# Output projection over 128 rows with the mask on zero weights, and a gate with its 8 columns standing

## The chip, the cores and the metric

One core of one Trainium2 chip. The time is device microseconds (us) of one execution of the whole kernel; lower is better. The three timed executions of the kernel before took 962.52, 965.40 and 968.63 us.

## The reference

Four residual steps on `x` of shape (8, 128, 512), fp32: a grouped-query attention, a dense layer with four routed low-rank adapters, a patchwise attention, and a mixture of 8 experts of which each token takes 2. The change touches the third step's last product and the fourth step's gate:

```python
def _L1_xattn_ref(qk, v, masks, Wq, bq, Wk, bk, Wv, bv, Wo, bo):
    ...
    o = jnp.einsum('bhij,bhdj->bhdi', attn, vh).reshape(BN, DK, W)      # DK = 64
    o = jax.nn.gelu(o, approximate=False)
    out = jnp.einsum('de,bew->bdw', Wo, o) + bo[:, None]
    out = out.reshape(B, np_, D, W).transpose(0, 2, 1, 3).reshape(B, D, S)
    out = out * masks
    return out

def _L1_ffn_ref(x, W_gate, b_gate, W_e, b_e):
    TOP_K = 2
    logits = x @ W_gate + b_gate                                        # (8, 128, 8)
    _, top_idx = jax.lax.top_k(logits, TOP_K)
    y_all = jax.nn.relu(jnp.einsum('bsd,edh->bseh', x, W_e) + b_e)
    y = jnp.take_along_axis(y_all, top_idx[..., None], axis=2)
    return y.mean(axis=2)

x = x + jnp.tanh(g_xattn[1]) * _L1_xattn_ref(_layernorm(x), ctx, mask, ...)
x = x + jnp.tanh(g_ffn[1]) * _L1_ffn_ref(_layernorm(x), ...)
```

## The kernel before

`x` stays in SBUF as `X`, 8 batches of 128 tokens by 512. Each engine has its program written out by hand (a block each for SyncE `sp`, GpSimd `gp`, ScalarE `ac`, VectorE `ve`, TensorE `pe`); engines meet through semaphores, and an engine runs its own instructions in the order in which they are written. The four residual steps follow one another, and the loops inside run over batches.

The place of the change is the stretch between the patchwise attention and the experts. A batch passes through these steps there:

- ScalarE's `gelu(b)` (L866) works on `o_t[0:64, b, :]`, the 64 attention channels of a batch, and GpSimd's `masked(b)` (L626) multiplies them by the mask. Row 64 of `o_t` holds the mask itself (loaded by SyncE, L403), so that the bias row of the weights `wo1g` is masked as well.
- TensorE's `output(b)` (L1670) is one fp32 product over 65 rows into bank 2 or 3. In the trace it has two instruction records.
- VectorE's `attended(b)` adds it to `X` (L1210) and takes the statistics of the row (`row_stats`, L911 and L914); GpSimd's `row_scale` turns them into mean and 1/sigma (L496 to L499); `final_rows(b)` normalises into `h` or `h2` (L917). SyncE writes that out to `h_rows` (`keep_rows`, L449). From batch 4 on, `final_rows` waits until the first four batches are written out (`hrow_out`).
- TensorE's `turn_last(b)` transposes the normalised batch in four pieces (L1677), and ScalarE evicts it to `xt` (L877). After each such eviction ScalarE also rounds two pieces of the expert weights (`expert_hi`, L683).
- TensorE's `gate(b)` (L1683) multiplies each of the four pieces of `xt`, 128 by 128 and standing in the array, by 8 streaming columns of `wg`. The 128 by 8 logits of four batches lie side by side in one bank.
- VectorE, behind its last `final_rows`, copies `tri` (L1233), then runs `choose(0)` and `choose(1)` (L1240 to L1255), which rank the logits of four batches each. Then come the counting products (L1701 to L1709), the list of rows per expert tile, the gather from `h_rows` and the expert products.

TensorE's order is written out: outputs 0 to 2, then per turn `output(b)`, `turn_last(b - 3)`, `gate(b - 4)`.

Two other places are touched. VectorE makes `wo1g` inside the second step (L1181, in the turn of batch 3), and TensorE waits soon after it for `p_w` and `h`, which VectorE writes behind it (L917). SyncE's queue issues, in that order, the context load of batch 2 (L397), the copies of `stack(2)` (L421 to L430, for which the scores of batch 2 wait) and a load of expert weights (L407).

Of the kernel before, what the change touches and what calls it, by code (L numbers as in the profile page):

```python
# [46 lines left out]
def flamingo_gated_two_layers(nc, x, ctx, ctx_t, mask_tq, mask_b, g_xattn, g_ffn, wq0, wk0, wv0, wo0,  # L47
# [6 lines left out]
    with ExitStack() as stack:  # L54
# [69 lines left out]
        diag = sb("diag", [P, HG + 1])  # L124
        wo1g = sb("wo1g", [E1 + 1, P])
        wg = sb("wg", [P, KT, EX])
# [122 lines left out]
        mask_8 = over("mask_8", [B, D])  # L249
        o_t = sb("o_t", [E1 + 1, B, D])  # L250
        ctx_s = sb("ctx_s", [P, 2, D])
# [86 lines left out]
        def _(sp):  # L338
# [57 lines left out]
            def load_ctx(b, j):  # L396
                sp.dma_start(ctx_s[:, j, :], ctx[b]).then_inc(ctxs_in[j], 16)  # L397
# [3 lines left out]
            for b in range(B):  # L401
                sp.dma_start(mask_bb[:, b, :], mask_b[b, 0:1, :].to_broadcast([P, D])).then_inc(maskb_in, 16)
            sp.dma_start(o_t[E1:E1 + 1, :, :], mask_b.rearrange("b o d -> o b d")).then_inc(maskb_in, 16)  # L403
            sp.dma_start(mask_8[:, :], mask_b.rearrange("b o d -> (b o) d")).then_inc(pen_raw, 16)
# [31 lines left out]
            for b in range(2, B):  # L436
                sp.wait_ge(vc_mm, CREDIT + b - 1)
                load_ctx(b, b % 2)
                stack(b)
                if b - 2 < FIRST:  # L440
                    load_expert(b - 2)
# [42 lines left out]
        def _(gp):  # L484
# [139 lines left out]
            def masked(b):  # L624
                gp.wait_ge(gelu_ok, CREDIT + b + 1)
                nc.gpsimd.tensor_tensor(o_t[0:E1, b, :], o_t[0:E1, b, :], mask_bb[0:E1, b, :], ALU.mult).then_inc(om_ok, 1)  # L626

            masked(0)
            masked(1)
# [35 lines left out]
        def _(ac):  # L665
# [194 lines left out]
            def expert_hi(e, k):  # L860
                if k == 0:
                    ac.wait_ge(we_in[e], 16)
                hi_part(w_hi[:, e, k, :], w_raw[e][:, k, :], weh_ok)

            def gelu(b):
                nc.scalar.activation(o_t[0:E1, b, :], o_t[0:E1, b, :], ACT.Gelu).then_inc(gelu_ok, 1)  # L866
# [8 lines left out]
            for b in range(B):  # L875
                ac.wait_ge(ht_mm, CREDIT + 2 * B + b + 1)
                nc.scalar.activation(xt[:, :, b * P:(b + 1) * P], heads(ps[:, b % 2, :]), ACT.Copy).then_inc(hth_ok, 1)  # L877
                for n in range(2 * b, 2 * b + 2):
                    expert_hi(n // KT, n % KT)
# [23 lines left out]
        def _(ve):  # L903
# [273 lines left out]
            for b in range(2, B):  # L1177
                mix(b, b % 2, last=b == B - 1)
                row_stats(2, b - 2, b % 2, x2_ok)
                if b == 3:  # L1180
                    nc.vector.tensor_scalar(wo1g[:, :], wo1[:, :], tanh_g[0:E1 + 1, 1:2], None, ALU.mult).then_inc(wo1_ok, 1)  # L1181
                    nc.vector.memset(q3[PARTS:PARTS + 1, :, :, :].bitcast(F32), 1.0).then_inc(pen_ok, 1)
# [5 lines left out]
                if b == B - 5:  # L1188
                    ve.wait_ge(maskb_in, 16 * (B + 1))
                    rows(0, 0, p_w)  # L1190
                    kept(0, 0)
# [43 lines left out]
            def choose(half):  # L1235
# [3 lines left out]
                ve.wait_ge(gate_mm, CREDIT + 4 * half + 4)  # L1239
                nc.vector.tensor_tensor(gl[:, at, :], ps[:, 4 + half, 0:4 * EX].rearrange("p (b e) -> p b e", b=4),  # L1240
                                        bcast(bg[:, :], 4), ALU.add).then_inc(rank_ok, 1)
# [121 lines left out]
        def _(pe):  # L1363
# [316 lines left out]
            def gate(b):  # L1680
                pe.wait_ge(hth_ok, CREDIT + 2 * B + b + 1)
                for k in range(KT):
                    last = nc.tensor.matmul(ps[:, 4 + b // 4, b % 4 * EX:(b % 4 + 1) * EX], xt[:, k, b * P:(b + 1) * P], wg[:, k, :],  # L1683
                                            start=k == 0, stop=k == KT - 1)
                last.then_inc(gate_mm, 1)

            pe.wait_ge(wo1_ok, CREDIT + 1)
            for b in range(3):
                output(b, b % 2)
            for b in range(3, B + 3):  # L1690
# [3 lines left out]
                if b >= 4:  # L1694
                    gate(b - 4)
            gate(B - 1)

            pe.wait_ge(kz_ok, CREDIT + 1)
# [106 lines left out]
```

## Time and profile before

| what | us |
|---|---|
| median of three timed executions | 965.40 |
| lowest and highest of them | 962.52, 968.63 |
| the profiled execution, whole | 966.84 |
| its span in the trace | 965.0 |
| TensorE busy | 894.5 |
| VectorE busy | 619.6 |
| ScalarE busy | 325.0 |
| GpSimd busy | 404.5 |

All times inside the trace are counted from the start of the span of the one profiled execution; the 1.84 us between span and whole execution lie around it. TensorE's products overlap one another, so the length of a single record is longer than its step to the next one: where a rate matters, the chain of waits shows the step. PE in the views is TensorE, PEld its weight loads, DVE is VectorE, ACT ScalarE, POOL GpSimd, SPq the queue that SyncE issues to. PEclk is the granted clock of TensorE as a share of 2.4 GHz; 0.50 is 1.2 GHz.

### The profile page before, as it was taken

What the parts mean: (1) busy time and instruction counts of PE and PEld (TensorE: products, weight loads), DVE (VectorE), ACT (ScalarE), POOL (GpSimd) and SP (SyncE); (2) the same over time, 40 slices, a digit from 0 to 9 for tenths busy, and PEclk for the clock granted to TensorE, in tenths of its full rate; (3) what the DMA queues carried; (4) which work ended last, traced back from release to release, by engine and by line L of the source; (5) the groups of instructions that cost most, each with busy time, mean ns of one, the idle gap of its engine ahead of it and who ended that gap; (6) DMA issues with size and microseconds to landing.
All of it is one profiled execution on the core that took longest, in us unless ns stands there. A gap on an engine that the chain in (4) does not pass through costs nothing.

```text
span 965.0 us, 13870 instructions
## 1 busy us (share of the span) xinstructions
PE 894.5 (93%) x4771; PEld 728.3 (75%) x4771; DVE 619.6 (64%) x1067; ACT 325.0 (34%) x581; POOL 404.5 (42%) x417
## 2 busy tenths in 40 slices
PE   5999999999999999999999999988999998857993
PEld 4778878978878877877977877865888885745772
DVE  5975675375674276575376577578888875777345
ACT  4333143223133214124214124221665664612230
POOL 4651532251442153253153153337764606528551
PEclk9999999999999999999999999989999996559997
DMA  9020120020120011120011011202344205313448
GB/s 314 11 88 1 33 88 1 12 87 2 33 88 1 13 45 43 33 88 1 12 43 44 1 27 52 87 26 61 113 136 134 66 2 214 142 44 131 134 149 307
DMA packets 42242, 70.13 MB, mean 73 GB/s; under 512 B 7034, under 2 KB 14779, under 8 KB 42051
## 3 DMA queue, kind: packets, MB, share of 16 engines
q1 hardware_dynamic: 37060, 56.97, 18.1%
q0 software_dynamic: 3680, 12.06, 3.8%
q8 instruction: 43, 0.70, 0.3%
q10 hardware_dynamic: 1440, 0.24, 0.1%
q14 instruction: 19, 0.16, 0.1%
HBM read 52.61 MB, written 10.22 MB: 65 GB/s over the span
## 4 chain that ended last, share of the span: by engine, by line
PE 84%; DVE 8%; issue 3%; DMA 2%; ACT 1%; ACTq 1%; POOL 1%; DVEq 0%; SPq 0%
PE ps L1370 18%; PE ps L1372 18%; PE ps L1371 17%; PE ps L1491 6%; PE ps L1483 6%; PE ps L1620 5%; PE ps L1499 3%; PE ps L1608 3%; PE ps L1601 2%; PE ps L1670 1%; DMA rows_in<-h_rows,gather_i 1%; PE ps L1716 1%; PE ps L1628 1%; DVE h L917 1%; PE ps L1576 1%
## 5 line engine op out<-in xcount | busy, mean ns | idle before, releaser
L528 POOL TENSOR_TENSOR q_t<-rot_a,rot_b 128x512 f32<-128x512 f32 x64 | 82.7, 1291 | 152.8 <-DVE rot_b L962 152.8
L960 DVE TENSOR_TENSOR rot_a<-ps,cos 128x512 f32<-128x512 f32 x80 | 55.2, 689 | 87.2 <-PE ps L1372 86.6
L1370 PE MATMUL ps<-xt_hi,wq_hi 128*128 128x512 f32 x256 | 107.6, 420 | 0.5 <-DVE rot_b L962 0.5
L1370 PE MATMUL ps<-wo_hi,at_hi 128*128 128x512 f32 x256 | 106.7, 417 | 0.4 <-DVE at_lo L1068 0.4
L1372 PE MATMUL ps<-xt_hi,wq_lo 128*128 128x512 f32 x256 | 101.1, 395 | 0.0
L1371 PE MATMUL ps<-xt_lo,wq_hi 128*128 128x512 f32 x256 | 101.0, 394 | 0.0
L1372 PE MATMUL ps<-wo_hi,at_lo 128*128 128x512 f32 x256 | 100.2, 391 | 0.0
L1371 PE MATMUL ps<-wo_lo,at_hi 128*128 128x512 f32 x256 | 99.9, 390 | 0.0
L755 ACT ACTIVATE ps<-ps 128x512 f32<-128x512 f32 x64 | 37.2, 582 | 178.6 <-PE ps L1483 178.6
L768 ACT ACTIVATE at_hi<-ps 128x512 fp32r<-128x512 f32 x64 | 38.2, 597 | 171.7 <-PE ps L1499 171.7
L1073 DVE TENSOR_TENSOR X<-ps,X 128x512 f32<-128x512 f32 x64 | 44.2, 690 | 74.0 <-PE ps L1372 73.7
L592 POOL TENSOR_TENSOR k_blk<-k,diag 96x512 fp32r<-96x512 f32 x64 | 65.4, 1053 | 24.7 <-DMA k<-qk_lo 24.7
L502 POOL TENSOR_TENSOR wq_lo<-wq_raw,wq_hi 128x512 fp32r<-128x512 f32 x32 | 41.4, 1297 | 78.8 <-ACT wq_hi L683 78.8
L1370 PEld LDWEIGHTS ps<-wo_hi,at_hi 128*128 128x128 f32 x256 | 48.0, 187 | 30.3 <-DVE at_lo L1068 17.2
L1491 PE MATMUL ps<-v_ones,e_w 128*128 128x129 f32 x512 | 67.7, 275 | 0.0
L528 POOL TENSOR_TENSOR k_t<-rot_a,rot_b 128x512 f32<-128x512 f32 x16 | 20.7, 1294 | 108.5 <-DVE rot_b L962 108.5
L1620 PE MATMUL ps<-v_pad,p_t 128*128 128x72 f32 x512 | 64.8, 269 | 1.1 <-ACT p_t L836 1.0
L1068 DVE TENSOR_TENSOR at_lo<-ps,at_hi 128x512 fp32r<-128x512 f32 x64 | 44.2, 690 | 32.6 <-ACT at_hi L768 32.6
L1483 PE MATMUL ps<-q_t,k_t 128*128 128x512 f32 x128 | 64.1, 593 | 0.0
L1491 PEld LDWEIGHTS ps<-v_ones,e_w 128*128 128x128 f32 x512 | 62.8, 192 | 0.7
L1620 PEld LDWEIGHTS ps<-v_pad,p_t 128*128 128x128 f32 x512 | 62.2, 192 | 1.4 <-ACT p_t L836 1.1
L1051 DVE TENSOR_TENSOR e_w<-ps,cap 128x512 f32<-128x512 f32 x64 | 44.1, 689 | 28.8 <-ACT ps L757 28.5
(217 smaller groups left out, 2131.2 us busy)
## 6 DMA issues: line engine op xcount, KB each, us to landing
wq_raw<-in_wq SPq DMA_DIRECT2D x8, 1024.0 KB, 5.2
wo_raw<-in_wo SPq DMA_DIRECT2D x8, 1024.0 KB, 5.1
w_raw<-in_we SPq DMA_DIRECT2D x8, 1024.0 KB, 5.7
X<-in_x SPq DMA_DIRECT2D x4, 512.0 KB, 11.9
wk_raw<-in_wk SPq DMA_DIRECT2D x8, 256.0 KB, 2.9
q_t<-in_ctx_t SPq DMA_DIRECT2D x2, 1024.0 KB, 9.5
wv_raw<-in_wv SPq DMA_DIRECT2D x4, 512.0 KB, 3.7
ctx_s<-in_ctx SPq DMA_DIRECT2D x8, 256.0 KB, 4.2
```

The source lines that it names most:

```text
L528: nc.gpsimd.tensor_tensor(dst, rot_a[:, r % 2, :], rot_b[:, r % 2, :], ALU.add).then_inc(rope_ok, 1)
L592: nc.gpsimd.tensor_tensor(k_blk[0:PARTS, b % 2, g, patch, :, :], bcast(k3[0:PARTS, g, patch * P:(patch + 1) * P].bitcast(F32), HG), diag[0 ...
L960: nc.vector.tensor_tensor(heads(rot_a[:, r % 2, :]), heads(bank), bcast(cos[:, :], 4), ALU.mult)
L1051: nc.vector.tensor_tensor(heads(e_w[:, b % 2, :]), heads(ps[:, 2 + b % 2, :]), bcast(cap[:, :], G), ALU.min).then_inc(e_ok, 1)
L1068: nc.vector.tensor_tensor(at_lo[:, b % 2, :], ps[:, 6, :], at_hi[:, b % 2, :].bitcast(F32), ALU.subtract).then_inc(al_ok, 1)
L1073: nc.vector.tensor_tensor(X[:, b, :], ps[:, 7, :], X[:, b, :], ALU.add).then_inc(x1_ok, 1)
L1370: nc.tensor.matmul(dst, w_hi, x_hi, start=start and k == 0, stop=False)
L1371: nc.tensor.matmul(dst, w_hi, x_lo, start=False, stop=False)
L1372: last = nc.tensor.matmul(dst, w_lo, x_hi, start=False, stop=stop and k == n - 1)
L1483: nc.tensor.matmul(ps[:, 2 + b % 2, :], k_t[:, b * P:(b + 1) * P], q_t[:, :, b * P:(b + 1) * P], start=True, stop=True).then_inc(s_mm, 1)
L1491: last = nc.tensor.matmul(ps[:, 4 + n // 2, at:at + P + 1], e_w[:, b % 2, n * P:(n + 1) * P], v_ones[:, b, 1 if odd else 0, 0:P + 1], star ...
L1620: last = nc.tensor.matmul(ps[:, 6 + j, patch * VA:(patch + 1) * VA], p_t[:, u % 2, n * P:(n + 1) * P], v_pad[:, at:at + VA], start=head == ...
```

## The change

`o_t` and `wo1g` become 128 rows high. VectorE first clears rows 64 to 127 of `wo1g`, then writes rows 0 to 64 as before, so that rows 65 to 127 hold zeros. Rows 64 to 127 of `o_t` hold the mask, one copy from DRAM with 64 partitions as destination instead of one; it is issued later, behind the context load of batch 2, and counts on `pen_raw`, for which GpSimd now waits ahead of `masked(0)`. The product of `output(b)` runs over 128 rows.

The gate is turned round: `wg[:, k, :]`, 128 by 8, stands in the array and a batch's 128 columns of `xt` stream, which gives logits of 8 by 128 in bank 4 or 5. ScalarE evicts them to `r_d` (`gate_row`), and TensorE transposes that into the place in which `choose` wants them (`gate_columns`, now banks 6 and 7).

```diff
-        wo1g = sb("wo1g", [E1 + 1, P])
+        wo1g = sb("wo1g", [P, P])
...
-        o_t = sb("o_t", [E1 + 1, B, D])
+        o_t = sb("o_t", [P, B, D])
...
-            sp.dma_start(o_t[E1:E1 + 1, :, :], mask_b.rearrange("b o d -> o b d")).then_inc(maskb_in, 16)
...
                 load_ctx(b, b % 2)
+                if b == 2:
+                    sp.dma_start(o_t[E1:P, :, :], mask_b.rearrange("b o d -> o b d").to_broadcast([P - E1, B, D])).then_inc(pen_raw, 16)
                 stack(b)
...
+            gp.wait_ge(pen_raw, 32)
             masked(0)
...
+            def gate_row(b):
+                ac.wait_ge(ot_mm, CREDIT + B + b + 1)
+                nc.scalar.activation(r_d[0:EX, b // 4, b % 4 * P:(b % 4 + 1) * P], ps[0:EX, 4 + b % 2, 0:P], ACT.Copy).then_inc(ot_ev, 1)
...
                 nc.scalar.activation(xt[:, :, b * P:(b + 1) * P], heads(ps[:, b % 2, :]), ACT.Copy).then_inc(hth_ok, 1)
+                if b >= 1:
+                    gate_row(b - 1)
+                if b == B - 1:
+                    gate_row(b)
                 for n in range(2 * b, 2 * b + 2):
                     expert_hi(n // KT, n % KT)
...
-                    nc.vector.tensor_scalar(wo1g[:, :], wo1[:, :], tanh_g[0:E1 + 1, 1:2], None, ALU.mult).then_inc(wo1_ok, 1)
+                    nc.vector.memset(wo1g[E1:P, :], 0.0).then_inc(wo1_ok, 1)
+                    ve.wait_ge(wo1_ok, CREDIT + 1)
+                    nc.vector.tensor_scalar(wo1g[0:E1 + 1, :], wo1[:, :], tanh_g[0:E1 + 1, 1:2], None, ALU.mult).then_inc(wo1_ok, 1)
...
-                    ve.wait_ge(maskb_in, 16 * (B + 1))
+                    ve.wait_ge(maskb_in, 16 * B)
...
-                nc.vector.tensor_tensor(gl[:, at, :], ps[:, 4 + half, 0:4 * EX].rearrange("p (b e) -> p b e", b=4),
+                nc.vector.tensor_tensor(gl[:, at, :], ps[:, 6 + half, 0:4 * EX].rearrange("p (b e) -> p b e", b=4),
...
-                    last = nc.tensor.matmul(ps[:, 4 + b // 4, b % 4 * EX:(b % 4 + 1) * EX], xt[:, k, b * P:(b + 1) * P], wg[:, k, :],
+                    last = nc.tensor.matmul(ps[0:EX, 4 + b % 2, 0:P], wg[:, k, :], xt[:, k, b * P:(b + 1) * P],
                                             start=k == 0, stop=k == KT - 1)
-                last.then_inc(gate_mm, 1)
-
-            pe.wait_ge(wo1_ok, CREDIT + 1)
+                last.then_inc(ot_mm, 1)
+
+            def gate_columns(b):
+                pe.wait_ge(ot_ev, CREDIT + B - 1 + b + 1)
+                nc.tensor.transpose(ps[:, 6 + b // 4, b % 4 * EX:(b % 4 + 1) * EX], r_d[0:EX, b // 4, b % 4 * P:(b % 4 + 1) * P],
+                                    ident[0:EX, 0:EX]).then_inc(gate_mm, 1)
+
+            pe.wait_ge(wo1_ok, CREDIT + 2)
...
                 if b >= 4:
                     gate(b - 4)
+                if b >= 5:
+                    gate_columns(b - 5)
             gate(B - 1)
+            gate_columns(B - 2)
+            gate_columns(B - 1)
```

On TensorE, in the mixed stage (batches 6 and 7 of `output`; `h_149` is `h2`), there stood before:

```order
L1670 MATMUL ps<-o_t,wo1g 128x512 [waits x3_ok,om_ok]
L1677 MATMUL ps<-ident,h_149 128x128 [waits hth_ok,h_ok]
L1677 MATMUL ps<-ident,h_149 128x128 x3
L1683 MATMUL ps<-wg,xt 128x8 [waits hth_ok]
L1683 MATMUL ps<-wg,xt 128x8 x3
L1670 MATMUL ps<-o_t,wo1g 128x512 [waits x3_ok,om_ok]
```

and there stands now, at the same place:

```order
L1682 MATMUL ps<-o_t,wo1g 128x512 [waits x3_ok,om_ok]
L1689 MATMUL ps<-ident,h_149 128x128 [waits hth_ok,h_ok]
L1689 MATMUL ps<-ident,h_149 128x128 x3
L1695 MATMUL ps<-xt,wg 8x128 [waits hth_ok]
L1695 MATMUL ps<-xt,wg 8x128 x3
L1701 MATMUL ps<-ident,r_d 128x8 [waits ot_ev]
L1682 MATMUL ps<-o_t,wo1g 128x512 [waits x3_ok,om_ok]
```

The four gate products write 8 by 128 where they wrote 128 by 8, and one transpose, of the batch before, stands behind them ahead of the next output.

On ScalarE, the evictions of `xt` in the same stage with the expert weights between them (`w_raw_138` is expert 1), before:

```order
L877 ACTIVATE xt<-ps 128x4x128 [waits ht_mm]
L683 ACTIVATE w_hi<-w_raw_138 128x512 [waits we_in1]
L683 ACTIVATE w_hi<-w_raw_138 128x512
L877 ACTIVATE xt<-ps 128x4x128 [waits ht_mm]
L683 ACTIVATE w_hi<-w_raw_138 128x512 x2
```

and now:

```order
L883 ACTIVATE xt<-ps 128x4x128 [waits ht_mm]
L869 ACTIVATE r_d<-ps 8x128 [waits ot_mm]
L685 ACTIVATE w_hi<-w_raw_138 128x512 [waits we_in1]
L685 ACTIVATE w_hi<-w_raw_138 128x512
L883 ACTIVATE xt<-ps 128x4x128 [waits ht_mm]
L869 ACTIVATE r_d<-ps 8x128 [waits ot_mm]
L685 ACTIVATE w_hi<-w_raw_138 128x512 x2
```

Behind each eviction of `xt` stands one of a batch's logits, which waits for the gate of the batch before.

## Rows read from the trace of the kernel before

**Rows 1.** The page: busy time by engine, TensorE's granted clock by slice

```profile
PE 894.5 (93%) x4771; PEld 728.3 (75%) x4771; DVE 619.6 (64%) x1067; ACT 325.0 (34%) x581; POOL 404.5 (42%) x417
...
PEclk9999999999999999999999999989999996559997
```

**Rows 2.** Chain of waits: start us, us, engine, tile and line (x instruction records)

```profile
745.12 1.02 PE ps L1628 x8
...
752.84 0.86 PE ps L1576 x2
753.70 0.44 PE ps L1608 x4
...
801.20 1.92 PE ps L1628 x8
803.12 5.43 PE ps L1670 x6
...
814.94 1.51 PE ps L1683 x8
816.44 1.91 PE ps L1670 x2
...
826.92 0.70 DVE X L1210
...
831.42 1.21 DVE tri L1233
...
842.89 0.39 PE ps L1701
```

**Rows 3.** Stretches: length, busy PE PEld DVE ACT POOL (x), PEclk, DMA share, GB/s

```profile
671.70:675.00 3.30, 3.27 (x8) 2.06 (x9) 3.20 (x8) 0.55 (x1) 0.83 (x4) 0.50 0.34 86
675.00:680.00 5.00, 4.92 (x42) 4.52 (x41) 4.78 (x8) 3.61 (x7) 5.00 (x8) 1.00 0.34 91
676.80:683.80 7.00, 7.00 (x62) 6.74 (x60) 6.64 (x12) 4.79 (x10) 7.00 (x9) 1.00 0.13 39
803.10:808.60 5.50, 5.44 (x7) 1.75 (x6) 3.16 (x7) 0.59 (x1) 1.72 (x4) 0.50 0.74 246
811.00:838.40 27.40, 27.11 (x105) 22.36 (x104) 19.26 (x30) 14.68 (x28) 18.57 (x29) 0.50 0.41 155
```

**Rows 4.** Timeline of TensorE: start us, us, line, out<-in, shapes

```profile
672.29 1.91 PE L1576 MATMUL ps<-h,wqk 128*128 128x512 f32 x2
673.99 1.06 PE L1608 MATMUL ps<-ident,p_w 128*128 128x128 f32 x4
```

**Rows 5.** Groups by line, 801 to 843 us: count, busy us, mean ns, idle before

```profile
L917 DVE TENSOR_SCALAR h<-X,mean,rstd 128x512 f32<-128x512 f32 x8 | 5.9, 747 | 0.4 <-POOL rstd L499 0.4
L911 DVE BATCH_NORM_STATS2 stats<-X 128x6 f32<-128x512 f32 x8 | 5.6, 695 | 0.3
L1210 DVE TENSOR_TENSOR X<-ps,X 128x512 f32<-128x512 f32 x8 | 5.5, 690 | 11.4 <-PE ps L1670 11.3
...
L914 DVE BATCH_NORM_AGGREGATE mean_var<-stats 128x2 f32<-128x6 f32 x8 | 1.5, 182 | 0.3
```

**Rows 6.** Timeline of VectorE

```profile
811.13 0.68 DVE L1210 TENSOR_TENSOR X<-ps,X 128x512 f32<-128x512 f32 x1
...
839.39 0.18 DVE L1240 TENSOR_TENSOR gl<-ps,bg 128x32 f32<-128x32 f32 x1
```

**Rows 7.** DMA issues from 795 to 870 us: count, KB each, median us to landing

```profile
h_rows<-h SPq DMA_DIRECT2D x8, 256.0 KB, 2.2
```

**Rows 8.** VectorE, the line that clears a tile: ns min/median/max, start

```profile
L943 DVE MEMSET count<- x1: 72/72/72, 19.8 to 19.8; 128x16 f32 x1
```

**Rows 9.** VectorE, the line that writes wo1g

```profile
L1181 DVE TENSOR_SCALAR wo1g<-wo,tanh_g x1: 704/704/704, 637.0 to 637.0; 65x128 f32<-65x128 f32 x1
```

**Rows 10.** Timeline of SyncE's queue, its issues

```profile
676.32 0.52 SPq L397 DMA_DIRECT2D ctx_s<-in_ctx  x1
683.87 2.60 SPq L421 DMA_DIRECT2D k<-qk_hi  x4
```

## The prediction, made before the changed kernel was run

> **What bounds the kernel now.** I read four views in this order. First the page: TensorE is busy for 93% of the span, at the higher of its two clock levels, 2.4 GHz, almost everywhere; the three slices that say 6, 5, 5 lie between about 796 and 868 us [rows 1]. The reader is to see that the one long dip is exactly where the change works. Second, the chain of waits there: from 803.12 to 826.92 it is TensorE's (outputs L1670, transposes L1677, gate L1683), then VectorE's from its last addition of a projected batch at 826.92, through `tri` at 831.42, up to TensorE's L1701 at 842.89 [rows 2]. So what matters in this stage is when VectorE gets the last output, not when the last gate is done. Third, the table by stretches: the clock is 0.50 (1.2 GHz) from 803.1 to 838.4, although TensorE is busy for 5.44 of the first 5.50 us and nearly all the time afterwards [rows 3]. Fourth, the groups: L1210 of VectorE waits 11.3 us for TensorE in total and works 5.5 [rows 5]; the other engine has much room.
>
> What the clock did before it rose elsewhere is the key. At 671.7 it was at 0.50 too. Then came two records of a 128-row, 512-column fp32 product and 128-row transposes [rows 4], in a stretch with 3.27 of 3.30 us busy, and from 675 it is 1.00 [rows 3]. At 803.12 the same kind of product with 65 rows ran 5.43 us without a pause [rows 2], and nothing rose. The visible difference between the two is the rows: 128 against 65. This is an inference from one place each, not a proof.
>
> A rule of the Trainium skill speaks against the change: "TensorE: Matmul & The Clock Gate", Part 1 (The HAM clock gate), says that the gate follows how busy the array has been, with sustained back-to-back work releasing it, and names no rows. By that rule padding rows would buy nothing. The trace of 803.1 to 808.6 does not fit a rule of busy time alone, so I lean on rows; what the rule would give is the first rival. The same page, Part 4 (PE-mode transpose), says that transposes don't count as busy for the gate; no row here separates that, and it would leave outputs and gate alone to hold the clock.
>
> **The change, part by part.**
>
> *Outputs with 128 rows.* Eight products, each 2 records. At the low clock three of them took 5.43 us, 1.81 each; the number of rows does not set that: the 128-row product in rows 4 took 1.91 for its two records at the low clock, the 65-row one also 1.91, and the 128-row one 0.86 at the high clock [rows 2, 4]. So padding alone costs nothing, and the clock gives back 1.91 - 0.86 = 1.05 per output. I expect outputs 0 to 2 still at 1.2 GHz, with the rise near their end, about 808.
>
> *Gate turned round.* Before: 4 products with 8 columns streaming, 1.51 us per batch at 1.2 GHz [rows 2]. After: 4 products with 128 columns streaming. The nearest row is L1628, also 4 fp32 products of 128 columns: 1.92 us at 1.2 GHz and 1.02 at 2.4 [rows 2]. To this comes one small transpose per batch for the columns; its price is bounded by 0 and by the 0.44 that four 128x128 transposes take at the high clock [rows 2]; a quarter of that is 0.11, and I take 0.15, and 0.2 at the low clock. So a gate costs 1.17 at the high clock and 2.12 at the low one, 0.6 more than before. ScalarE gets an eviction of 8x128 per batch. It was busy for 14.68 of the 27.40 us from 811 to 838.4 [rows 3], and the eviction sits beside TensorE's next products, except after the last batch, where VectorE has not reached the second `choose` yet. Its price is not shown; bounds are the 0.18 of a tiny VectorE operation and the 0.69 of a 128x512 one [rows 5], and I take 0.3.
>
> *The rate per batch.* TensorE at 2.4 GHz: 0.86 + 0.44 + 1.02 + 0.15 = 2.47 us. Before, at 1.2 GHz: 1.91 + 2 x 0.44 + 1.51 = 4.30; the additions of batches 3 and 7 began 826.92 - 811.13 = 15.8 us apart, 3.95 a batch, since the first of the four has no gate ahead of it. VectorE: 0.69 + 0.70 + 0.18 + 0.75 = 2.32 [rows 5]. The two are almost level; 2.47 is the larger and sets the pace. VectorE's addition of batch 3 began at 811.13 [rows 6], and there it was VectorE's own work that was late, so it stays. Four more batches: 811.13 + 4 x 2.47 = 821.0 instead of 826.92, 5.9 us earlier. What is late next is VectorE, at 2.32. One wait could come forward: `final_rows(4)` needs the fourth copy into h_rows landed, 2.2 us after its issue [rows 7]; the fourth normalised batch is ready near 818, so landing near 820.5, about when VectorE comes to it: 0 to 0.5, held within the 5.9. If that cover were gone, each further microsecond of landing would be one of the time.
>
> *After the last addition.* The chain is VectorE's to 842.89 in both kernels: 16 us from 826.92, unchanged in work. The gates have to be done by `choose(1)`, 839.39 before [rows 6], which moves to 833.5; TensorE, with 1.17 + 0.44 per batch left, is done by about 830. TensorE then idles and falls back to 1.2 GHz as before; the routing and expert stage moves as a whole by 5.9 us.
>
> *The transfer.* The 1-row copy into `o_t` goes from SyncE's queue; a 64-partition one (1 MB) comes behind the context load of batch 2, issued at 676.32. SyncE's next issue was at 683.87 [rows 10], and the DMA engines were busy for 0.13 of 676.8 to 683.8 [rows 3]. At the rate of 803.1 to 808.6, where 246 GB/s kept the engines busy for 0.74 [rows 3], 1 MB needs 1 / 0.33 = 3.2 us and fits. Behind it on the queue stands `stack(2)`, on which scores of batch 2 hang; without that gap it would be up to 3 us later. I take 0. POOL's new wait before `masked(0)` is for this copy, which is some 120 us old by then: 0. Behind it on POOL stand all of `masked`, and thus all outputs.
>
> *memset of 64x128, and a wait, on VectorE* near 637, ahead of `p_w` and `h` for which TensorE waits soon after. Bounds: 0.07 (128x16 cleared) [rows 8] and 0.70 (all of wo1g) [rows 9]; I take 0.2, nearer to the first since it is a clear. It is on the path.
>
> **Sum:** -5.9 + 0.2 = -5.7 us. The profiled execution took 966.84 us (span 965.0 and 1.84 around it): 961.1. It lies 1.4 above the median of 965.4, so in the terms of the median 965.4 - 5.7 = 959.7, 0.6% faster.
>
> **Rivals.**
> 1. *The clock never rises (slower): the change doesn't do what it looks made to do.* Something other than the rows kept the clock at 0.50 from 803 on, and keeps it there. For it: the work before 803.12 and the wait behind it are the same in both kernels, and the mixed stage from 811 to 838.4 was busy for 27.11 of 27.40 us without a rise [rows 3]. Against it: the pair of places above. The Trainium skill's rule of busy time (above) gives the same outcome, since nothing is made busier. The price: 0.6 per gate. Three gates with their small transposes stand before the last addition, +1.8; all eight before `choose(1)`: TensorE's work reached to about 838.4 [rows 3], 1.0 us ahead of `choose(1)` [rows 6], so 8 x 0.6 + 0.3 for ScalarE's last eviction - 1.0 = 4.1 late, which takes in the 1.8. It decides from the point where the last gate is done after `choose(0)`. 965.4 + 4.1 + 0.2 = 969.7.
> 2. *It rises and falls again.* Outputs bring it up, then gates with 8 columns standing, or transposes, don't hold it. For it: a stage of transposes and gates never rose before (811 to 838.4 at 0.50) [rows 3]. Against: in the attention stage before, made of short products and transposes, the clock stayed at 9 tenths or more for four slices [rows 1], and every batch here still has a full output. At two of the four batches each way: gain 2.9, extra cost 2 x 0.6 = 1.2: 965.4 - 1.7 + 0.2 = 963.9.
> 3. *It rises at once, or never falls.* For it: the fall came only about 801, and where it comes may differ from one execution to another. Against: nothing in the change touches what went before 803. Output 0 is done 1.81 - 0.86 = 0.95 earlier, and VectorE, whose own work sets the pace from there to 811.13, starts that much earlier: 959.7 - 0.95 = 958.7.
>
> **How the numbers follow.** Forecast 0.65, rival 1 0.13, rival 2 0.12, rival 3 0.10. The forecast's own range: at best a batch costs 0.86 + 0.44 + 0.86, a gate priced like one output and no transpose, 2.16 x 4, 1.2 us more gained; at worst the clock rises one batch late, 1.8 us less: 958.5 to 961.5. The executions of before lie between 962.5 and 968.6, so 3 us either way are spread that no term explains. I give 956.0 to 967.5, which takes in rivals 2 and 3 and leaves out most of rival 1. A measurement of this kernel tells about 1% from no change. Over 1% faster means below 955.7, which needs more than VectorE's own pace allows: 0.1. Over 1% slower needs 975.1: 0.03. Within 1%: 0.87.
>
> **What would show it.** Right: granted clock 1.00 from about 808 to after 825, output records near 0.43 us apart instead of 0.9, gates near 1.0 us per batch, VectorE's last addition of a projected batch near 821, and L1701's counterpart near 837. Wrong: clock 0.50 up to 838 with gates of 1.9 us (rival 1), a table in which the clock goes up and down within the stage (rival 2), TensorE waiting for scores of batch 2 near 690 (the transfer), or VectorE waiting on h_rows by more than 1 us. The sum is wrong if the clock rises and the last addition still comes after 823.

## The result, and the profile after

The changed kernel takes 959.5 us (median of 7, 957.4 to 960.0) against 964.5 for the kernel before in the same measurement: 0.9941 of it, interval 0.9917 to 0.9965. Measured again later beside other kernels it came to 957.2 against 962.9, 0.9933 [0.9911, 0.9955]. The forecast was 959.7 against 965.4, 0.9941. The direction, the size and the main mechanism hold; the reservation is the turned gate, which the rest shows to be worth nothing that can be measured beside the rows. In a later measurement one execution of a variant took 1480 us and one of the kernel before 3085; both are left out of the ratios.

The page of the kernel after, the lines that answer to [rows 1]:

```profile
span 955.4 us, 13896 instructions
...
PE 879.5 (92%) x4779; PEld 713.1 (75%) x4779; DVE 622.6 (65%) x1068; ACT 326.7 (34%) x589; POOL 404.7 (42%) x417
...
PEclk9999999999999999999999999999999999859997
```

TensorE has 8 instructions more and 15 us less to do. The low slices of 6, 5, 5 have shrunk to 8, 5. The stretches of the stage (length, then busy us of TensorE, its weight loads, VectorE, ScalarE, GpSimd, then granted clock, DMA share, GB/s), beside [rows 3]:

```profile
798.30:801.70 3.40, 3.40 (x9) 1.98 (x8) 0.14 (x1) 1.19 (x3) 0.86 (x1) 0.51 0.27 75
801.80:829.00 27.20, 20.43 (x118) 11.50 (x116) 24.55 (x38) 16.25 (x35) 22.38 (x37) 1.00 0.66 245
829.10:856.00 26.90, 11.89 (x43) 10.10 (x44) 21.44 (x54) 7.99 (x16) 7.80 (x7) 0.50 0.29 99
```

Before, 27.4 us of this stage ran at 0.50 with TensorE busy for 27.11. Now 27.2 us run at 1.00 with TensorE busy for only 20.43: it has gaps, and VectorE, busy for 24.55, is nearly the bound. The timeline of TensorE shows the rise and the new step (start, us, line, tiles, shapes; in brackets the idle time ahead):

```profile
799.45 4.04 PE L1682 MATMUL ps<-o_t,wo1g 128*128 128x512 f32 x6
805.37 1.12 PE L1682 MATMUL ps<-o_t,wo1g 128*128 128x512 f32 x2 [1.88 <-POOL o_t L627]
...
814.04 1.13 PE L1682 MATMUL ps<-o_t,wo1g 128*128 128x512 f32 x2
815.01 0.60 PE L1689 MATMUL ps<-ident,h 128*128 128x128 f32 x4
815.54 1.04 PE L1695 MATMUL ps<-xt,wg 128*8 128x128 f32 x8
816.51 0.22 PE L1701 MATMUL ps<-ident,r_d 8*128 8x8 f32 x1
816.66 1.13 PE L1682 MATMUL ps<-o_t,wo1g 128*128 128x512 f32 x2
```

Output 0 began at 799.45 with the clock at 0.50; the clock rose at 801.6. From 814.04 to 816.66 one turn takes 2.62 us: output 0.97, transposes 0.53, gate 0.97, small transpose 0.15. VectorE's additions, answering to [rows 6]:

```profile
801.55 0.69 DVE L1222 TENSOR_TENSOR X<-ps,X 128x512 f32<-128x512 f32 x1 [3.75 <-PE ps L1682]
...
807.52 0.68 DVE L1222 TENSOR_TENSOR X<-ps,X 128x512 f32<-128x512 f32 x1
...
815.21 0.69 DVE L1222 TENSOR_TENSOR X<-ps,X 128x512 f32<-128x512 f32 x1 [0.55 <-PE ps L1682]
...
817.82 0.69 DVE L1222 TENSOR_TENSOR X<-ps,X 128x512 f32<-128x512 f32 x1 [0.49 <-PE ps L1682]
```

VectorE still waits for TensorE, but by half a us per batch. The statistics and normalising between the additions are left out of the lines. And the chain behind the last addition, answering to the end of [rows 2]:

```profile
817.82 0.70 DVE X L1222
...
822.32 1.21 DVE tri L1245
...
833.77 0.39 PE ps L1722
...
840.14 3.60 PE ps L1730 x16
```

Where did the profiled 9.6 us between the spans (965.0 and 955.4) go? Three pieces. (1) The first addition came at 801.55 instead of 805.16: 3.6 us, earned before the changed stage. TensorE began the last transposes before it at 797.86 instead of 801.20. VectorE was already 1.9 us ahead when it reached the code that writes `wo1g` (statistics at 634.30 instead of 636.23), and a dip of the clock that follows near 645 lasted 3.4 us instead of 6.7; a second one near 670 lasted 3.4 in both. That is spread between executions: two variants below whose code up to output 0 is that of the kernel before, the filler kernels, began output 0 at 799.39 and 799.42, where the kernel before began it at 803.05. (2) From the first addition to the last 16.27 us instead of 21.76: 5.5 us, the change. (3) From the last addition to the counting products 15.95 against 15.97: nothing, and 0.5 us less in all that follows. So of a difference that looks like 9.6, the change owns 5.5, and 5.5 of 965 is the measured 0.6%.

### The profile page after: what moved, and what is told of

Its sections match the earlier page's. It is cut to its first block, busy times and chain, and to the rows that moved or that the text cites. A ratio compares the mean times of both kernels' runs of the same rounds, so it can differ in the third digit from the quotient of the medians.

```text
span 955.4 us, 13896 instructions
## 1 busy us (share of the span) xinstructions
PE 879.5 (92%) x4779; PEld 713.1 (75%) x4779; DVE 622.6 (65%) x1068; ACT 326.7 (34%) x589; POOL 404.7 (42%) x417
## 4 chain that ended last, share of the span: by engine, by line
PE 77%; DVE 10%; POOL 4%; issue 4%; DMA 3%; ACT 1%; ACTq 0%; SPq 0%; DVEq 0%; POOLq 0%
PE ps L1382 18%; PE ps L1384 17%; PE ps L1383 17%; PE ps L1503 6%; PE ps L1495 6%; PE ps L1632 3%; PE ps L1511 3%; POOL k_blk L593 3%; DMA rows_in<-h_rows,gather_i 2%; PE ps L1620 2%; PE ps L1613 1%; DVE stats L921 1%; PE ps L1737 1%; DVE h L927 1%; DMA rb<-in_router_b 1%
## 5 line engine op out<-in xcount | busy, mean ns | idle before, releaser
L503 POOL TENSOR_TENSOR wq_lo<-wq_raw,wq_hi 128x512 fp32r<-128x512 f32 x32 | 41.4, 1297 | 78.9 <-ACT wq_hi L685 78.9
```

## The experiments

Stages are compared by the distance from VectorE's first addition to its last, since that is free of what went before. The kernel before takes 21.76 us there, the changed one 16.27.

**One edit at a time.** First the 128 rows alone, with the old gate; the diff is against the changed kernel:

```diff
-                    last = nc.tensor.matmul(ps[0:EX, 4 + b % 2, 0:P], wg[:, k, :], xt[:, k, b * P:(b + 1) * P],
+                    last = nc.tensor.matmul(ps[:, 4 + b // 4, b % 4 * EX:(b % 4 + 1) * EX], xt[:, k, b * P:(b + 1) * P], wg[:, k, :],
...
-                if b >= 1:
-                    gate_row(b - 1)
...
-                if b >= 5:
-                    gate_columns(b - 5)
```

> Outputs over 128 rows as in the changed kernel, gate as before (8 columns streaming). Rows theory: the clock rises within the first three outputs (near 802 to 808 us of the span, the last output record ends near the changed kernel's); if short gates don't hold it, it falls again inside the mixed stage, and the time is between the two, 961 to 964 against 964.5 before. If gates don't matter for the clock, all of the gain is here: a gate at 2.4 GHz is about 0.8 us against 1.0, and the time is 958.5 to 960. Rival (it is the turned gate that keeps the clock up): no rise at all, 0.50 to the end of the stage, 964 to 965.

Measured: 958.9 against 963.3, 0.9948 [0.9925, 0.9972]; the stage took 16.17 us. The rows alone give all that this measurement can tell from the whole change. The stretches of this kernel (same columns as above):

```profile
807.30:810.70 3.40, 3.40 (x13) 2.16 (x11) 2.87 (x6) 1.93 (x4) 3.40 (x6) 0.50 1.05 408
810.80:821.00 10.20, 9.38 (x65) 7.13 (x65) 8.27 (x17) 7.25 (x15) 6.79 (x16) 1.00 0.66 246
821.10:833.00 11.90, 5.75 (x29) 5.68 (x28) 11.48 (x16) 11.28 (x23) 9.68 (x8) 0.50 0.54 210
```

The clock was at 1.00 when output 0 began, fell at 807.3 and was back at 810.7, with 128-row outputs and old gates. It fell again at 821.0, behind the last output, while three of the eight gates were still to come. In the changed kernel it fell only at 828.9, when TensorE was done (826.8). So turned gates kept the clock up behind the last output and the old ones didn't, but nothing waited for that: VectorE reached its second ranking at 829.51, behind the last slow gate. VectorE also waited 0.4 us here for the copies into `h_rows` to land, the wait that the prediction had named.

The traces show one execution each. The mean granted clock of every execution is on record, too: 0.963 to 0.971 in the 12 of this kernel, 0.972 to 0.975 in 13 of the changed one, and 0.951 to 0.964 in 92 of the kernel before (at most 0.961 beside this one).

Then the turned gate alone, with 65-row outputs, again against the changed kernel:

```diff
-        o_t = sb("o_t", [P, B, D])
+        o_t = sb("o_t", [E1 + 1, B, D])
...
-        wo1g = sb("wo1g", [P, P])
+        wo1g = sb("wo1g", [E1 + 1, P])
```

> Outputs over 65 rows as before, gate turned round (128 columns streaming, 8 standing). Rows theory: outputs 0 to 2 run at 1.81 us each and the clock is still 0.50 when the mixed stage begins. Then either it stays there, and gates at 1.9 us put the last logits behind the second choose: 3 to 5 us slower than before, 968 to 970; or the gates with 128 columns streaming raise it, in the mixed stage only, and the time lies at 960 to 964. Rival (the rise had nothing to do with the rows): the clock rises at outputs 0 to 2 as in the changed kernel, 959.5.

Measured: 961.0, 0.9969 [0.9953, 0.9986]; stage 20.31 us. The stretches of this kernel, same columns as above:

```profile
800.00:803.70 3.70, 2.60 (x6) 0.68 (x4) 2.88 (x6) 0.21 (x1) 1.31 (x4) 1.00 0.77 229
803.80:817.40 13.60, 12.69 (x36) 6.35 (x37) 9.00 (x17) 4.57 (x10) 10.47 (x21) 0.50 0.84 320
817.50:834.40 16.90, 11.63 (x79) 7.31 (x77) 14.78 (x20) 13.82 (x31) 12.77 (x14) 1.00 0.41 150
```

Outputs 0 to 2 were done at 1.00 here, and the clock fell during the pause behind them. It then stayed at 0.50 for 13.7 us, with TensorE busy for 12.69 of them, and rose at 817.4, behind the second turned gate. With 65-row outputs and the old gate it did not rise in the stage (before, and the two filler kernels below). So the turned gate is not only a price: beside 65-row outputs the clock rose with it, late, and the mean granted clock of all its twelve executions (0.966 to 0.973) lies above that of the kernel before. The prediction had not foreseen that; the expectation of this run had it as its second case. Its first premise, output 0 at a low clock, did not come about, since the clock was high there.

**What about the rows counts: the data, the transfer, or their number?** In the changed kernel, rows 65 to 127 of `o_t` are made zeros, and the transfer is gone (GpSimd copies the mask row itself). The output is unchanged, since the weights of these rows are zeros:

```diff
-                    sp.dma_start(o_t[E1:P, :, :], mask_b.rearrange("b o d -> o b d").to_broadcast([P - E1, B, D])).then_inc(pen_raw, 16)
...
+            nc.gpsimd.memset(o_t[E1:P, :, :], 0.0).then_inc(oz_ok, 1)
...
+            nc.gpsimd.tensor_copy(o_t[E1:E1 + 1, :, :], mask_bb[E1:E1 + 1, :, :]).then_inc(oz_ok, 1)
```

> The changed kernel with rows 65 to 127 of the streaming operand holding zeros instead of the mask's ones (GpSimd clears rows 64 to 127 and copies the mask into row 64 while it waits for the first gelu; no transfer). Rows as such: clock and time as in the changed kernel, 959.5 within 2 us. Rival (data that switches or is nonzero counts, not rows): outputs 0 to 2 stay at 1.8 us each and the clock is 0.50 at 806 us; 962 to 969.

Measured: 957.9, 0.9948 [0.9928, 0.9967]; stage 17.05. Its stretches:

```profile
803.40:805.20 1.80, 1.80 (x3) 0.84 (x3) 0.00 (x0) 0.59 (x1) 0.00 (x0) 0.50 0.31 36
805.30:812.20 6.90, 3.84 (x12) 1.35 (x11) 6.44 (x11) 0.00 (x0) 4.95 (x11) 0.99 0.98 354
812.30:815.50 3.20, 3.20 (x10) 1.24 (x9) 2.85 (x5) 2.12 (x4) 3.20 (x5) 0.50 1.05 408
815.60:836.00 20.40, 15.12 (x100) 9.47 (x98) 17.30 (x26) 16.28 (x37) 16.32 (x23) 1.00 0.51 190
```

Output 0 began at 803.46, at 0.50, and the clock rose 1.9 us later, as with the mask in the rows. Zero rows are as good; and taking the transfer away gained nothing, which is the only test made of its price. The table also shows a fall (812.3) behind the waits of 1.88 and 1.16 us between outputs 2 and 4, and the clock was back 3.4 us later.

A size between, 96 rows (the transfer and the clearing end at row 96 too):

```diff
-        o_t = sb("o_t", [P, B, D])
+        o_t = sb("o_t", [96, B, D])
...
-        wo1g = sb("wo1g", [P, P])
+        wo1g = sb("wo1g", [96, P])
```

> The changed kernel with 96 instead of 128 rows in outputs. If a third quarter of the rows is enough, clock and time as in the changed kernel, 959.5 within 2 us; if it is not, outputs 0 to 2 run at 1.8 us each with the clock at 0.50, and it rises late or not at all: 962 to 969.

Measured: 961.8, 0.9977 [0.9956, 0.9998]. Its one profiled execution looks like the changed kernel (stage 16.98, a fall at 806.2 and a rise at 809.6), its median doesn't. But whole times say little here: the profiled execution with zero rows took 963.2 us and this one 956.5, with stages of 17.05 and 16.98. The mean granted clock was 0.965 to 0.974 in the ten executions, above every one of the kernel before in this measurement (0.951 to 0.961). Whether 96 rows raise the clock less surely than 128 is left open.

**The same fillers with 128 rows and with 65.** This pair holds busy time equal. The kernel before, with three unread products in TensorE's waits behind outputs 2 and 3, once of 128 rows and once of 65; nothing reads them, and the gate writes bank 4 anew:

```diff
+            def spin(n):
+                for _ in range(n):
+                    nc.tensor.matmul(ps[:, 4, :], wqk1[:, :], mask_bb[:, 2, :], start=True, stop=True)
...
+            spin(2)
...
+                if b == 3:
+                    spin(1)
```

(the other has `wo1g[:, :], o_t[:, 2, :]` as its operands)

> The kernel before, its outputs at 65 rows and its gate unturned, with unread products of 128 rows (wqk1 standing, a batch of the mask streaming, 512 columns): two behind output 2 and one behind output 3, where TensorE waits in any case. Rows raise the clock: if the clock is at 0.50 when output 2 ends, it is 1.00 about 2 us after the first of them begins. What follows tells whether 65-row outputs and gates of 8 streaming columns hold it: if they do, the last addition comes some 16 us after the first as in the changed kernel, and the time is near 0.995 of before; if 65 rows don't count for holding either, the clock falls again within the stage, the last addition comes 20 to 22 us after the first, and the time is 0.998 to 1.00. The rival, that something else than rows kept the clock down here, expects no rise at all: 0.50 to 838, and up to 2 us slower since products of 1.9 us stand in the waits.

> The same as the run with 128-row fillers, but the unread products have 65 rows (wo1g standing, batch 2 of o_t streaming). If what raises the clock is how busy TensorE is, it rises here as there, since the fillers close the same waits. If it is the rows, the clock stays as the kernel before has it: at 0.50 through the whole stage where it was at 0.50 at its start, the last addition 21.8 to 23 us after the first, ratio 1.00 (0.998 to 1.002).

Measured: 961.8, 0.9990 [0.9974, 1.0007] with 128 rows, and 964.7, 1.0026 [1.0002, 1.0049] with 65. The two executions that were profiled reach the stage within 0.03 us of each other, both with the clock at 1.00. TensorE's timeline with 128-row fillers (L1690):

```profile
799.39 3.10 PE L1670 MATMUL ps<-o_t,wo1g 65*128 65x512 f32 x6
802.32 1.88 PE L1690 MATMUL ps<-mask_bb,wqk 128*128 128x512 f32 x4
804.37 1.12 PE L1670 MATMUL ps<-o_t,wo1g 65*128 65x512 f32 x2 [0.17 <-POOL o_t L626]
805.33 1.02 PE L1690 MATMUL ps<-mask_bb,wqk 128*128 128x512 f32 x2
806.66 0.66 PE L1677 MATMUL ps<-ident,h 128*128 128x128 f32 x4 [0.30 <-DVE h L917]
...
818.57 2.05 PE L1670 MATMUL ps<-o_t,wo1g 65*128 65x512 f32 x2
```

and with 65-row fillers:

```profile
799.42 3.10 PE L1670 MATMUL ps<-o_t,wo1g 65*128 65x512 f32 x6
802.35 1.88 PE L1690 MATMUL ps<-o_t,wo1g 65*128 65x512 f32 x4
804.39 1.12 PE L1670 MATMUL ps<-o_t,wo1g 65*128 65x512 f32 x2 [0.16 <-POOL o_t L626]
805.35 1.02 PE L1690 MATMUL ps<-o_t,wo1g 65*128 65x512 f32 x2
806.68 1.04 PE L1677 MATMUL ps<-ident,h 128*128 128x128 f32 x4 [0.31 <-DVE h L917]
```

Up to 806.7 the rows of the two agree in every start and duration to 0.03 us; they differ in the height of the fillers and in what these read. Then the transposes take 0.66 in the one and 1.04 in the other. The stretches of both, first the one with 128-row fillers:

```profile
799.40:806.70 7.30, 6.82 (x16) 2.45 (x15) 5.94 (x11) 0.61 (x2) 4.65 (x11) 1.00 0.79 265
806.80:810.20 3.40, 2.70 (x19) 1.88 (x18) 3.26 (x7) 2.27 (x5) 3.40 (x6) 1.00 1.06 410
810.30:830.00 19.70, 19.70 (x79) 16.24 (x78) 13.58 (x21) 10.19 (x20) 12.51 (x20) 0.50 0.41 157
```

and with 65-row fillers:

```profile
799.40:806.70 7.30, 6.81 (x16) 2.44 (x15) 5.92 (x11) 0.63 (x2) 4.64 (x11) 1.00 0.78 273
806.80:810.20 3.40, 3.40 (x12) 2.21 (x12) 2.68 (x6) 1.63 (x3) 3.40 (x6) 0.50 1.05 407
```

With 6.82 and 6.81 us of 7.30 busy, the clock fell at 806.8 with 65-row fillers and at 810.35 with 128-row ones. Busy time alone does not tell the two apart. The fillers differ in their height, and also in what they read (weights and mask in the one, `wo1g` and an output's operand in the other); the run with zero rows speaks against the data as the reason, but the two differences were not taken apart here. And with 65-row outputs and the old gate afterwards, TensorE was busy for all of 19.70 us at 0.50 in both kernels and nothing rose. Fillers in the waits cost nothing that was measured at 128 rows, but did not hold the clock behind them; the outputs themselves need the rows.

Whether fillers raise the clock could not be tested, since it was high when they began. A rise is tested by setting the 65-row filler kernel beside the one with the rows alone: same old gate, clock high at output 0 in both, a fall at 806.8 in the one and 807.3 in the other, and TensorE busy without a pause for the next 3.4 us (3.40 of 3.40 in both). With 128-row outputs the clock was back at 810.7. With 65-row outputs:

```profile
810.30:830.00 19.70, 19.70 (x76) 16.28 (x77) 12.44 (x21) 9.81 (x18) 10.96 (x19) 0.50 0.41 154
```

"TensorE: Matmul & The Clock Gate", Part 1 (The HAM clock gate), in the Trainium skill explains the clock by how busy the array was. The two filler kernels, equal in busy time as the profile's rows count it, do not agree with that.

**Three attempts at more.** First, the same fillers of 128 rows in the changed kernel, against the fall between outputs 2 and 4:

```diff
+                    nc.tensor.matmul(ps[:, 4, :], wo1g[:, :], o_t[:, 2, :], start=True, stop=True)
```

> The changed kernel with three products whose result nobody reads, two behind output 2 and one behind output 3, where TensorE otherwise waits for VectorE and GpSimd. Theory: the clock falls in some executions because of those waits (seen near 807 in three of the runs so far); with the gaps filled it stays at 1.00 from the outputs to the end of the stage, whatever it did before them, and the time is 957 to 959.5 with a smaller spread. Rival (the fall there costs nothing, since VectorE sets the pace at that place): same time as the changed kernel, 958 to 960, or 0.5 to 1 longer if a filler delays output 3.

Measured: 957.6 against 962.9, 0.9943 [0.9920, 0.9966]; all eight additions stand at the same times as in the changed kernel to 0.01 us. No gain, and the spread did not shrink (954.4 to 959.6). In both profiled executions the clock had fallen before the stage and risen at outputs 0 to 2, so there was no later fall to mend.

Second, `tri` copied between the last two projected batches, where VectorE waits, instead of behind them:

```diff
+                if b == B - 2:
+                    ve.wait_ge(route_in, 32)
+                    nc.vector.tensor_copy(tri[:, :], tri_raw[:, :]).then_inc(tri_ok, 1)
             final_rows(B - 2, 0)
             final_rows(B - 1, 1)
-            ve.wait_ge(route_in, 32)
-            nc.vector.tensor_copy(tri[:, :], tri_raw[:, :]).then_inc(tri_ok, 1)
```

> The changed kernel with VectorE's copy of tri moved from behind the last normalised batch to between batches 6 and 7, into a wait for TensorE of about 0.5 us. Theory (behind the last addition the path is VectorE's alone): the copy's 1.2 us leave it, 0.2 to 0.6 come back before the addition of batch 7: 0.6 to 1.0 less, ratio to the kernel before 0.993. Rival (the last logits or GpSimd end the stage): no gain, 959.5.

Measured: 0.9963 [0.9945, 0.9982]. From the last addition to the counting products 15.79 instead of 15.95: a miss. The chain of this kernel shows why:

```profile
820.93 1.28 DVE rank_b L1258
822.21 1.42 DVE rank_a L1259
823.62 1.42 DVE rank_b L1261
825.06 1.39 DVE rank_a L1264
...
830.49 0.34 DVE rank_b L1261
830.86 0.43 DVE rank_a L1264
```

L1261 takes 1.42 us the first time and 0.34 the second, on the same shapes. In between GpSimd's last eight subtractions of expert weights (L503, 819.25 to 830.2, some 1.37 each) have ended. While they run, VectorE gets through about one of its longer operations per subtraction. The copy took 0.22 us in its new place instead of 1.21, but the second run of L1259 took 1.41 instead of the 0.34 of its counterpart in the changed kernel: the time that the copy left went to the next operation.

Third, therefore, these eight subtractions behind `choose`:

```diff
+            gp.wait_ge(sel_ok, CREDIT + 2)
             for n in range(2 * KT, 4 * KT):
                 expert_lo(n // KT, n % KT)
```

> As e6, and GpSimd's eight subtractions for experts 2 and 3 wait until both rankings of logits are done. Theory: VectorE's ranking operations took 1.3 to 1.4 us each while GpSimd worked and 0.34 to 0.43 when it did not; alone they take 0.4, choose(0) 2.6 instead of 6.4, and TensorE's last logits become the limit: L1722's counterpart about 3.5 to 4.5 us earlier after the last addition, 955 to 956.5. Rival: GpSimd's 10.8 us then collide with the operations behind, or end after the list of rows is ready, and what was gained is given back: 958 to 960.

Measured: 959.4, 0.9965 [0.9943, 0.9987]. Its chain:

```profile
830.76 0.43 DVE rank_b L1259
831.19 0.33 DVE rank_a L1260
831.52 0.35 DVE rank_b L1262
831.89 0.44 DVE rank_a L1265
...
838.07 1.61 DVE r_d L1300
...
844.56 3.60 PE ps L1732 x16
```

The ranking is now 4.3 us shorter (last addition at 821.50, counting products at 833.13: 11.63 instead of 15.95), and the list of rows behind it 5.1 longer (11.43 instead of 6.37 us to the products that list the rows, L1732), since the subtractions run beside it now: L1300 takes 1.61 where its counterpart took 0.59. The contention is moved and not removed, as the rival said. The half of the expectation that came true is that TensorE's last logits, at 830.5, now held up VectorE's second ranking (830.54).

The Trainium skill's "GPSIMD Engine Reference", section 1 (Specifications), says that GpSimd shares its SBUF interfaces with VectorE and that they collide where a VectorE instruction has two SBUF inputs or runs in a 2-port mode. The rows with two inputs agree (0.34 against 1.42 us). The copy of `tri`, with one input, was slow beside GpSimd as well (1.21 against 0.22 us); no run shows in which mode it ran.

Last, the rows alone with fillers and both moves:

```diff
+            spin(2)
...
+                if b == B - 2:
+                    ve.wait_ge(route_in, 32)
+                    nc.vector.tensor_copy(tri[:, :], tri_raw[:, :]).then_inc(tri_ok, 1)
...
+            gp.wait_ge(sel_ok, CREDIT + 2)
```

> Outputs over 128 rows, gate as in the kernel before (8 columns streaming), with the fillers of e5 and both moves of e7. Theory (the turned gate adds nothing once the outputs hold the clock): the same as e7 or up to 1 us better, 954 to 956.5. Rival (only turned gates hold the clock behind the last output, and the last logits now decide): the clock falls before the last gates, they take 1.6 us each, and the time is 1 to 2 us over e7.

Measured: 959.6, 0.9967 [0.9948, 0.9986]; the 954 to 956.5 expected is missed. The stage itself is the shortest of all (15.70 us from first to last addition), and the list stage gives it back as in the run before. The rival's mechanism came in part: with the old gates the clock fell at 825.5, ahead of the last two gates, these took some 1.6 us each, and VectorE's second ranking waited for them. From the last addition to the counting products that cost 0.24 us against the run before (11.87 and 11.63), not 1 to 2. No kernel tried beats the changed one by more than the intervals.

**The changed kernel once more**, in one measurement with the two kernels of 65-row outputs:

> The changed kernel once more, beside the two below on the same chip, so that its time and stage can be compared with them. Both edits together are expected at 0.994 of the kernel before, as in the first measurement (0.9941); if the two edits gave independent gains, 0.9948 x 0.9969 = 0.9917 would be expected instead. Profile: whichever state the clock is in when output 0 begins, it is 1.00 from at most 2.5 us behind that start on, and at most one fall of about 3.3 us in the waits between outputs 2 and 4.

Measured: 957.2 against 962.9, 0.9933 [0.9911, 0.9955], stage 16.27. The product of the two single ratios, 0.9917, is at the edge of the interval of the first measurement and inside this one's, so the times alone don't decide whether the gains add. The stages say that they don't: 16.17 us with rows alone, 16.27 with both. In this execution the clock rose 2.8 us behind the start of output 0, a little later than the 2.5 expected.

Like with like, the turned gate even costs something in the stage. In the two profiles in which fillers kept the clock from falling there, it took 15.70 us with old gates, a wait of 0.5 us for `h_rows` and the moved copy of `tri` included, and 16.28 with turned ones. The whole times can't tell that from nothing.

## Why the prediction was right

- *Rows raise the clock.* Inferred from one place each; now borne out for a rise by the rows alone beside the 65-row fillers, for holding by the fillers of equal busy time, and for the data by the zero rows. Rows are not all that counts: turned gates beside 65-row outputs saw a rise, too. The rise was put at "about 808", with outputs 0 to 2 at 1.2 GHz. It came 2.2 us behind the start of output 0 (799.45 to 801.6), so that only output 0 and a part of output 1 were slow. That earned nothing, because VectorE sets the pace up to its fourth addition: 5.97 us from the first to the fourth in both kernels, as the forecast had it ("so it stays").
- *The rate per batch.* Forecast 2.47, measured 2.62. By the starts of the records, the output was taken at 0.86 and is 0.97, the transposes at 0.44 and are 0.53; the gate was taken at 1.02 and is 0.97; the small transpose is the 0.15 that was taken. Output and transposes were read from an attention stage; why they are longer here is not shown. From the fourth addition to the last 10.30 instead of the forecast 9.9 and 15.79 before.
- *ScalarE's eviction* 0.27 (0.3 taken), beside TensorE's work as forecast; the last small transpose was done at 826.8, and `choose(1)` began at 830.27.
- *The wait for `h_rows`* was put at 0 to 0.5 and did not show in the changed kernel. It came to 0.4 and 0.5 us in the two kernels with old gates and tall outputs, where VectorE got there sooner.
- *VectorE in `wo1g`.* +0.2 was forecast; the clear took 0.17 and the product 0.34 where it took 0.70 before, so in sum nothing. Why the product was shorter is not shown; that it made up for the clear is luck.
- *The transfer* at 0: issued at 673.59, SyncE's next issue at 680.58, 7.55 us behind the context load as in the kernel before; and without it the kernel is no faster.
- *The tail* "unchanged": 15.95 against 15.97.
- *Sum.* -5.9 forecast for the stage and -5.5 found; -5.7 in all and -5.0 to -5.8 measured. The mis-sized terms, 0.4 in the rate and 0.2 in `wo1g`, go against each other, so that the sum is closer than its terms. On the clock of the profile before, that is 3.6 us later, the last addition stands at 821.4 (forecast 821.0) and the counting products at 837.4 (837).

The rivals. The first (no rise) is refuted: in six profiles 128-row outputs began at a low clock, and it rose 1.8 to 2.8 us behind the start of output 0. The second (rises and falls again) holds in part: in five profiles of kernels with taller rows (rows alone, zero rows, 96 rows, and the two with `tri` moved and no fillers) the clock fell in TensorE's waits between outputs 2 and 4 and was up again 3.4 us later. VectorE sets the pace there, so it cost 0.7 to 0.8 us where the gate was turned too (stage 16.98 to 17.05 against 16.27) and not the 4.2 of that rival. In the two profiles with 128-row fillers and 128-row outputs it didn't fall there. The third (the clock may be high when output 0 begins) was seen in six of the thirteen profiles of this case; it moves the start of the stage, not its length.

One argument of the forecast was too simple: the turned gate was booked as a price of 0.6 us a batch at the low clock. At the high clock it costs 0.3 a batch (0.97 + 0.15 against the old gate's 0.82), of which VectorE's pace hides a part: 0.6 us are left over the stage (16.28 against 15.70). In exchange the clock rose with it beside 65-row outputs and stayed up behind the last output. Since the rows raise the clock sooner and nothing waits for the last gates, it adds nothing that can be measured here.

## What to carry to other kernels

Where TensorE is busy and its granted clock is yet at half, look at how many rows its products use and not only at how busy it is. Here a product over 65 rows took the same time as one over 128 at the same clock (1.91 us at 1.2 GHz), and padding it with zero weights gave the clock back 1.8 to 2.8 us behind the first output. Then take the second edit away again: the rows alone did all that was measured. Compare two executions by the distance between two events of the stage, and not by their spans: here 3.6 of 9.6 us were there before the stage began. And before moving work away from beside a slow VectorE operation, see what it will stand beside instead: an 11-us piece of GpSimd work slowed VectorE's longer operations in either place.

## What the runs showed of the hardware

- With equal busy time (6.8 of 7.3 us) the granted clock fell at 806.8 us with 65-row fillers and at 810.35 with 128-row ones. After a fall at about 807, with TensorE busy without a pause, it was back 3.4 us later with 128-row outputs and stayed at 0.50 for the rest of the stage with 65-row outputs. Rows of zeros did as well as others.
- Gates with 8 standing and 128 streaming columns, with 65-row outputs between, saw the clock rise after 13.7 us at 0.50; gates with 8 streaming columns in the same place saw no rise in 19.7 us of unbroken work. Behind the last output the clock stayed at 1.00 with the former until TensorE was done (828.9), and fell with the latter while gates were still to come (821.0).
- The clock's dips before the stage differ between executions of the same code: the kernel before had one of 6.7 us near 645 and one of 3.4 near 672, the filler kernels, the same up to there, a single one of 6.8 near 667. Output 0 began 3.7 us apart in them (803.05 and 799.4); whether the dips account for all of it is open.
- VectorE operations of 128x256 with two SBUF inputs took 0.34 to 0.43 us alone and 1.28 to 1.42 beside GpSimd's subtractions.
